# A gather by one-hot matmul in a graph network's second layer: three one-hot buffers built five steps ahead instead of two built three ahead, and picks that alternate between two PSUM banks

## What is computed

```python
h = relu(layernorm(x))
msg = h[src] * edge_weight                     # one row of 256 per edge
agg = segment_sum(msg, dst)                    # rows added up by destination node
out = x + concat([agg / max(deg, 1), h]) @ W.T + b
```

## Time and profile before

| | us |
|---|---|
| median of three runs | 1577.04 |
| lowest and highest of them | 1561.55, 1581.73 |
| the profiled execution | 1583.45 |
| its span, first to last instruction | 1581.6 |

### The profile page before, as it was taken

How to read it: one execution, slowest core, us unless ns; L and a number is a source line. 1 busy time by engine, 2 the same in 40 slices (tenths; PEclk the granted TensorE clock), 3 DMA queues, 4 the chain that set the end, 5 groups by cost and what they waited for, 6 DMA issues and landing times. The chain is left out here.

```text
span 1581.6 us, 22313 instructions
## 1 busy us (share of the span) xinstructions
PE 1247.6 (79%) x5244; PEld 935.1 (59%) x5244; DVE 1069.3 (68%) x2577; ACT 900.2 (57%) x2624; POOL 830.2 (52%) x863
## 2 busy tenths in 40 slices
PE   6874878878888788888888784588878887888877
PEld 5662666666666566666664462366666666666654
DVE  5761777778787777777877883456666556566656
ACT  2221776677777777767774472355555555455540
POOL 3026255556666656656660206366666566566660
PEclk9986998899999989989998897689999999899998
DMA  6146165556666666656663013133333333233332
GB/s 175 62 136 194 52 166 161 152 161 180 174 168 183 175 177 171 174 151 179 176 175 109 0 54 115 54 90 96 89 93 94 85 96 92 82 94 91 95 89 90
DMA packets 78863, 195.63 MB, mean 124 GB/s; under 512 B 15690, under 2 KB 34674, under 8 KB 78740
## 3 DMA queue, kind: packets, MB, share of 16 engines
q0 software_dynamic: 53952, 169.45, 38.8%
q1 hardware_dynamic: 21278, 21.56, 4.4%
q10 hardware_dynamic: 3510, 3.20, 0.6%
HBM read 180.92 MB, written 13.24 MB: 123 GB/s over the span
## 5 line engine op out<-in xcount | busy, mean ns | idle before, releaser
L734 POOL DMA_INDIRECT ring<-qv_tab,v_src x440 | 434.0, 986 | 368.6 <-PE bank L868 172.0
L1463 POOL DMA_INDIRECT y_ring<-y_tab,e_idx x380 | 371.3, 977 | 298.5 <-PE bank L1562 117.3
L795 ACT ACTIVATE ring<-ring 128x65 f32<-128x65 f32 x1720 | 431.7, 336 | 0.0
L1612 DVE SCALAR_TENSOR_TENSOR kx<-bank,rdeg,kx 128x256 f32 x440 | 212.6, 483 | 244.5 <-PE bank L1562 187.7
L1543 PE MATMUL bank<-y_parts,src_hot 128*128 128x512 f32 x900 | 285.0, 449 | 99.1 <-ACT src_hot L1498 35.2
L854 PE MATMUL bank<-kx,hotT 128*128 x880 | 261.7, 426 | 94.4 <-issue 49.1
L1497 ACT ACTIVATE src_hot<-src_off,piece_id 128x640 fp32r<-128x640 f32 x180 | 149.2, 829 | 259.7 <-PE bank L1543 125.8
L868 PE MATMUL bank<-ring,hot 128*128 128x265 f32 x880 | 280.7, 420 | 8.6 <-issue 5.8
L1562 PE MATMUL bank<-y_ring,hot 128*128 x880 | 252.2, 411 | 35.6 <-SPq L1486 13.4
L854 PEld LDWEIGHTS bank<-kx,hotT 128*128 128x128 f32 x880 | 178.2, 211 | 156.1 <-issue 128.1
L1543 PEld LDWEIGHTS bank<-y_parts,src_hot 128*128 128x128 f32 x900 | 176.6, 201 | 153.5 <-issue 64.8
(11 more groups left out here) (269 smaller groups left out, 984.5 us busy)
## 6 DMA issues: line engine op xcount, KB each, us to landing
ring<-qv_tab,v_src POOLq DMA_INDIRECT x440
qv_tab<-qv_out SPq DMA_DIRECT2D x25, 264.0 KB, 2.0
y_ring<-y_tab,e_idx POOLq DMA_INDIRECT x380
y_tab<-acc SPq DMA_DIRECT2D x12, 256.0 KB, 2.7
out_dram<-kx ACTq DMA_DIRECT2D x24, 128.0 KB
xs<-in_x_dram SPq DMA_DIRECT2D x4, 640.0 KB, 13.3
kx<-in_x_dram SPq DMA_DIRECT2D x4, 640.0 KB
src_i<-in_src_dram SPq DMA_DIRECT2D x36, 64.0 KB
```

The lines of the kernel that those rows point to most:

```text
L734: pool.indirect_dma_start(one_step(r, 0, PITCH), None, qv_tab, bass.IndirectOffsetOnAxis(ap=v_src[:, r:r + 1], axis=0)).then_inc(got[r % R ...
L795: A.activation(part, part, ACT.Copy, scale=one_step(r, EX + h, EX + h + 1)).then_inc(scaled, 1)
L1463: pool.indirect_dma_start(y_ring[:, e % RH, :], None, y_tab, bass.IndirectOffsetOnAxis(ap=e_idx[:, e:e + 1], axis=0)).then_inc(y_got[e % R ...
L1612: V.scalar_tensor_tensor(row, bank[r % SB][:, 0:D], rdeg[:, bass.ds(tiles[r % U], 1)], row, ALU.mult, ALU.add).then_inc(sums_added, 1)
```

## The change

It widens `src_hot` from two buffers to three, orders each build five steps before its use instead of three, and gives pick k the bank 5 + k % 2, so that a pick's first piece waits for the `add_low` of the pick before the last one. `read_src` moves with the builds: READ grows from 25 to 27, so DVE does it in its turn for step e - 27. The list of picks begins at READ + 2, so it moves too: before it was 27, 38, ..., 412 (36 picks), and now it is 29, 40, ..., 403 (35 picks).

```diff
         AHEAD = [20, 18, 16, 14, 12]
-        READ = AHEAD[0] + 5
+        BUILT = 5
+        READ = AHEAD[0] + BUILT + 2
+        SRCS = 3
         BY_PE = list(range(READ + 2, ET - 2, EVERY))
...
-        src_hot = tb("src_hot", [P, 2, NB, P], F32R)
+        src_hot = tb("src_hot", [P, SRCS, NB, P], F32R)
...
+            def pick_bank(k):
+                return bank[5 + k % 2]
...
                 def build_src(k, q):
                     n = k * PIECES + q
                     act.wait_ge(src_read, k + 1)
-                    if n >= 2:
-                        act.wait_ge(src_hot_used, n - 1)
-                    apart.follow(A.activation(src_hot[:, n % 2, :, :], src_off[:, :, :], ACT.Square, bias=piece_id[:, q:q + 1], scale=-1.0))
-                    A.activation(src_hot[:, n % 2, :, :], src_hot[:, n % 2, :, :], ACT.Relu, bias=ones[:, 0:1], scale=-1.0).then_inc(src_hot_ready, 1)
+                    if n >= SRCS:
+                        act.wait_ge(src_hot_used, n - SRCS + 1)
+                    apart.follow(A.activation(src_hot[:, n % SRCS, :, :], src_off[:, :, :], ACT.Square, bias=piece_id[:, q:q + 1], scale=-1.0))
+                    A.activation(src_hot[:, n % SRCS, :, :], src_hot[:, n % SRCS, :, :], ACT.Relu, bias=ones[:, 0:1], scale=-1.0).then_inc(src_hot_ready, 1)
...
                 for r in range(STEPS):
-                    if r + 3 in piece_at:
-                        build_src(*piece_at[r + 3])
+                    if r + BUILT in piece_at:
+                        build_src(*piece_at[r + BUILT])
                     if r in last_piece_at:
...
-                        A.copy(y_ring[:, e % RH, :], bank[5][:, 0:D]).then_inc(high_copied, 1)
+                        A.copy(y_ring[:, e % RH, :], pick_bank(k)[:, 0:D]).then_inc(high_copied, 1)
...
-                    if q == 0 and k >= 1:
-                        pe.wait_ge(picked_added, k)
+                    if q == 0 and k >= 2:
+                        pe.wait_ge(picked_added, k - 1)
                     for j in range(NB):
                         T = q * NB + j
-                        last = T_.matmul(bank[5][:, 0:2 * D], src_hot[:, n % 2, j, :], y_parts[:, T, :], start=(T == 0), stop=(T == NT - 1))
+                        last = T_.matmul(pick_bank(k)[:, 0:2 * D], src_hot[:, n % SRCS, j, :], y_parts[:, T, :], start=(T == 0), stop=(T == NT - 1))
...
-                    V.tensor_tensor(row, row, bank[5][:, D:2 * D], ALU.add).then_inc(picked_added, 1)
+                    V.tensor_tensor(row, row, pick_bank(k)[:, D:2 * D], ALU.add).then_inc(picked_added, 1)
```

## The result

| | before, us | after, us |
|---|---|---|
| median of 20 runs each | 1574.19 | 1565.54 |
| lowest, highest | 1561.49, 1596.98 | 1549.57, 1600.49 |
| span of the profiled execution | 1581.6 | 1562.5 |

The ratio after / before is 0.992, with a 95% interval from 0.989 to 0.995. The change gains 0.8%, about 12 us, where 36 were forecast. It is a gain beyond doubt, but a third of the size.

The account below looks back on a forecast made before the run. The prediction took a cycle of POOL's issues and PE's late notices as the bound. Terms -35 (middle), +2 (copy) and -3 (one pick less) gave -36 us: 1547 against the profiled execution, 1541 against the median, range 1500 to 1585.

Parts of the forecast that it names:

- What bounds the kernel now: Second layer's middle: POOL's issues and PE's late notices form a cycle; 15.1 us per group, 11.2 if PE never waited.
- POOL's bound: Second layer's middle: ten indirect DMAs at 1.26 us, 12.6 us per group; the middle can't lose more than 90 us.
- The waits removed: PE before the picks: 30.9 us of waits for add_low go, and 26 of the 32.5 us for src_hot.
- Next come the five banks: PE before the steps: five PSUM banks stop it next, five steps ahead of DVE where the old wait allowed three.
- What of it reaches the end: Middle: of 62 us relieved on PE 35 reach the end, 22 by 67 POOL waits instead of 84, plus 13.
- a longer run of PE that makes the notices later: Sign that the prediction is wrong: late notices grow longer when PE runs longer; no size given.
- The 13 us for steps that PE had really not done yet: POOL's waits in the middle: those for PE's unfinished steps shrink by an estimated 13 us, part of the 35.
- The clock: PE in the middle: fewer pauses bring back between nothing and 20 us of 30, taken as 5.
- The copy behind two builds: ACT copies a finished pick behind two builds, so DVE may wait before add_low: +2 us, bounds 0 and 58.
- `read_src` two steps earlier: DVE's read_src and the last build both move by two steps, SP's index load has less time: 0 us.
- POOL's cycle sets the pace and nothing is gained in the middle: Rival: PE's waits only change name, only the saved pick remains: about 1574 us, range 1560 to 1585; chance 0.28.

Follow-up runs that it names:

- pool_plain: Changed kernel with POOL issuing plain DMAs of the same size in place of the indirect ones (output wrong), first kind of chip: 1414.05 us, ratio 0.898.
- sb4: Changed kernel with four sum banks instead of five, first kind of chip: 1565.55 us, ratio 0.992 to the kernel before.
- buf3_only: Kernel before plus only the third src_hot buffer and builds five steps ahead, one pick bank, first kind of chip: 1574.84 us, ratio 0.996.
- banks_only: Kernel before plus only the two alternating pick banks, two src_hot buffers and builds three ahead, first kind of chip: 1579.94 us, ratio 1.003.
- every9: Changed kernel with a pick every 9th edge tile (43 picks instead of 35), second kind of chip: 1304.07 us, ratio 1.006 to the kernel before.
- mixed: Changed kernel with plain DMAs from POOL for odd edge tiles only (odd tiles wrong), second kind of chip: 1254.61 us, ratio 0.969 to the kernel before.
- same_list: Changed kernel with the list of picks of before (36 from edge tile 27, not 35), first kind of chip: 1567.51 us, ratio 0.992.
- before_again: Kernel before, unchanged, timed and profiled on a chip of the second kind: 1295.42 us.

## Why the prediction was wrong

**What bounds the kernel now.** The view of PE was right: 11.2 us per group without waits, 11.4 measured once the indirect DMAs were gone. So was the source of the lateness, which `pool_plain` shows beside `sb4` on one chip. POOL's bound was put too high: ten DMAs per eleven steps, where the layer needs 9.5, 12.0 us at 1.26 each and not 12.6. That the first kind of chip is special was not to be seen in the trace of before.

**The waits removed.** Right: 72.6 us of waits in front of the picks became 1.4. That neither part gains alone was not said. The prediction added 30.9 and 26 as if they were independent; in `buf3_only` and `banks_only` the wait that is left grows by 18 us where 25 went, and by 28 where 31 went.

**Next come the five banks.** Right as the place, wrong as a cause. PE does wait at the rule of five banks, but `sb4` with four waits as long and takes as long.

**What of it reaches the end: the step that failed.** The term was 35 us, and the middle gave 10. The argument was that longer runs of POOL mean fewer pauses at 1.3 us each, 67 instead of 84. There were fewer, nearly as foreseen: 57 after PE's notices, and 72 with those labelled "remote", where it was 92. But POOL's idle time beyond its usual 0.30 per DMA fell little. Before it was 202.8 - 336 x 0.30 = 102 us, 82 without the 20.4 of the start; after it is 176.2 - 101 = 75 us. The saving is 6 us and not 22. Part of the pauses had only changed their label (releaser "remote": 11.8 us before, 26.6 after), and all pauses together became longer: 102 us in 92 times before, the start's left out, and 88.2 in 72 after, 1.11 against 1.22 us. The price per pause was too high as well: 1.3 us came from one pause, while the prediction's own mean of 1.07 less 0.30 is 0.8, and 17 pauses fewer at 0.8 are 13 us.

DVE tells the same. It waited for PE 165.7 us in 100 times before and 166.1 us in 77 times after (with "remote"): fewer waits, longer ones, and nothing saved. This is what the prediction named as its own sign of being wrong, a longer run of PE that makes the notices later. How it comes about is argued and not shown: a PE that runs further without notices lets POOL run longer, and both stall for longer. The 13 us for steps that PE had really not done yet were an estimate without a row, and the runs don't show them apart.

**The clock** went from 0.94 to 0.96. PE's busy time per step fell from 427.10 / 374 = 1.142 us to 420.40 / 372 = 1.130, worth 4.4 us over 374 steps, near the 5 us taken. Its pauses per step fell from 85.9 / 374 = 0.230 to 79.6 / 372 = 0.214, the other 6 us. Together they are the 10 us of the middle.

**The copy behind two builds** didn't stop DVE: 0.3 us before L1595. Only at `every9` did DVE wait for it, inside a kernel that PE bounds.

**`read_src` two steps earlier** was taken as nothing. On the first kind of chip it is. On the second the changed kernel waits there for SP's load of the indices, from 860 to 1240 us:

```profile
DVE src_off L1584 <- DMA src_i<-in_src_dram: 38.6, 15, 5.0
```

The kernel before has no such wait. SP issues this load in order behind the landings of the edge tiles, and POOL is only about 7 tiles ahead there. `mixed`, where POOL is no bound, has no such wait either. POOL itself never stops in that stretch, so it costs little or nothing.

**The rivals.** "POOL's cycle sets the pace and nothing is gained in the middle" (1560 to 1585) held the measured 1565.54, inside the range. But the 10 us are gained in the middle and not by the pick saved (`same_list`), so it is not right as it stood either. Its other claim, that PE's waits would only change name, nearly came true. On the second kind of chip nothing is gained: POOL holds the changed kernel where PE's waits held the one before. The rival had 0.28 and deserved the most. What spoke for it, waits recurring after every few DMAs, was on the page; what was set against it, that some groups of steps ran near 11 us, only showed that PE can run that fast for a while (the rows named for it cover less than 3 us and no whole group), not that POOL can follow: with 9.5 DMAs per group at 1.26 us it can't hold any pace under 12.0.

**What stays open.** Whether on the first kind of chip POOL with its pauses sets the pace or PE's work with the late notices added: a pick more often would tell and wasn't timed there. PE never waited for a landing in the middle of either kernel there, and POOL had come 24 to 26 edge tiles further than needed at step 240, so POOL's rate can act only through the notices and not by rows that are missing. How the indirect DMA delays notices, and why only on some chips, if it is the chips. Whether a notice is delayed by one indirect DMA or only by a run of them.

## What to carry to other kernels

When an engine waits for its neighbours by turns, add up its waits over all releasers before and after a change: if the sum nearly stays, the waits were a symptom, and what sets the pace is elsewhere. Look for an engine without waits: on the second kind of chip that was POOL, which issues the DMAs. Two buffers that each look like the limit may cover for each other, so test them together and apart. A price per pause is to be taken from the mean of all pauses and not from one. And before a gain is read off a trace, ask whether the stall belongs to the kernel or to where it ran: with the indirect form in place of the plain one the changed kernel took about 150 us more on one kind of chip; on the other it took about 40 us more than with every second DMA plain.

## What the runs showed of the hardware

- On the first kind of chip the completion of matmuls reached DVE, ACT and POOL up to several microseconds late while POOL issued indirect DMAs back to back (DVE idle 2.92 us, then released as POOL paused; ACT idle 4.54 us, its build 4.3 us after the modelled end of the matmul that it waits for). With plain DMAs of the same bytes on a chip of the same kind (`pool_plain`) DVE's longest wait for PE was 1.8 us, and none of 308 sums was over 1 us late.
- The kernel before takes 1574 to 1581 us on the first kind of chip and 1294 to 1296 on the second, with the same durations of one sum (483 ns) and one indirect DMA (974 and 971 ns). The waits between engines differ, and with them the granted clock of the middle (0.94 and 1.00). Of the 280 us about 160 lie ahead of the second layer (its first sum begins at 960 and 801 us), where another loop of indirect DMAs runs (L734); no run changed that one.
- A plain DMA of an edge tile took POOL 0.54 us (`pool_plain`), an indirect one 0.96 plus 0.30 before the next (`before_again`).
- From its first sum to its end the second layer took 450 us (`pool_plain`, first kind) and 452 us (`mixed`, second kind) with plain DMAs for all or half of the edge tiles.
